# A graph layer on one core: row sums of two batches turned by one set of multiplications

## The chip, the cores and the metric

The kernel runs on one core of one Trainium2 chip. The metric is the device time in microseconds of one execution. It is compared with the time of the kernel before, run on the same chip.

## What is computed

```python
h = relu(layernorm(x))                       # x: 16 x 512 x 128
A = [A1, A2, shifted, A1.T, A2.T, shifted.T, eye]       # here A1 and A2 are both adj
HW = einsum('bnf,rfo->rbno', h, W[:, :F]) + einsum('rd,rdo->ro', W_edges, W[:, F:])[:, None, None, :]
AHW = einsum('rbnm,rbmo->rbno', A, HW)
out = x + max(AHW, axis=0) + b
```

There are 16 batches of 512 nodes with 128 features and seven relations r. `shifted` moves whole batches (`jnp.roll` on the batch axis of a stack of identity matrices), so it is the identity in each batch. The constant of each relation, multiplied by adj, becomes that constant times the row sum of adj (and, for the transposed relations, the row sum of its transpose).

## The kernel before

Everything lies with the 128 features on the partitions and the 512 nodes along the free dimension. Matrix products are made with float32r operands: each operand is split into a rounded part (`_hi`) and the rest (`_lo`), and three multiplications (hi by hi, hi by lo, lo by hi) give one product.

One batch passes through these steps. SP loads x, adj and adjT (each of the latter 1 MB), the bias, and stores the output. ACT makes a_hi from adj in four pieces (`split_adj`, L422) and aT_hi from adjT in four pieces (`split_adjT`, L431). Each piece also leaves the row sums of its 128 rows in `sums`. DVE makes a_lo and aT_lo of the first two pieces (L596, L603), POOL those of the last two (L334, L341). ACT makes h (L443) and h_hi (L449), DVE h_lo.

TensorE then computes, for batch b and in this order: gT = aggregate of h with adj into `bank_gT` (L808 to L818, 12 multiplications); the turn of h into `bank_p1` (L741); g = aggregate with adjT into `bank_g` (L832 to L841, 12 multiplications); the turn of the row sums into `bank_p2` (`turn_sums`, L749, four multiplications of 128 columns); the three products of h (`product`, i = 0 to 2, three multiplications each, L870 to L872) into bank_p0, 1 and 2; four small multiplications that start the other products with constant times row sum (`add_sums`, L860); the four products of gT and g. Product 2 overwrites bank_p2, so it waits until ACT has copied the turned sums out of it to `sumsT` (`copy_sumsT`, L473). The products with the sums wait for `sumsT` and for g_lo.

POOL writes the row sums into `sum_parts` (`part_sums`, L307 and L311): for each of the four 128-node pieces 128 columns, made of four groups of 32 (adj twice, adjT twice). In a group only the first four columns are filled: hi, lo, hi, lo. The turn puts those columns on partitions, and `c_rows`, 32 rows for each relation, has the rounded constant in two of the rows and its rest in the next two, and zero elsewhere.

ACT copies gT, hT and g out of PSUM as gT_hi, hT_hi and g_hi (L461, L455, L467), and DVE subtracts for the lo parts. ACT begins `best` with the first product (L480), and DVE takes the maximum with the other six (L637, L640). POOL adds x and bias (L327).

Each engine runs its own list of instructions in the order in which the code issues them. Semaphores join the lists. In the loop over b ACT's order is: split_adj(b+1), gT_hi(b), hT_hi(b), standard deviation (b+2), h(b+1), g_hi(b), sumsT(b), best(b), split_adjT(b+1). POOL's is: o_sb(b-1), a_lo and aT_lo of b+1, part_sums(b+1), bias DMA. SP's is: load x(b+3), load adj(b+2), store(b-1), load bias(b+1), load adjT(b+2). The adj load of a batch waits, among others, for gT of the batch two before (`gT_psum`), the adjT load for g of it (`g_psum`). Buffers of adj, adjT, their hi and lo parts, sums and sum_parts are double.

Of the kernel before, what the change touches and what calls it, by code (L numbers as in the profile page):

```python
# [5 lines left out]
ALU = mybir.AluOpType  # L6
# [5 lines left out]
P = 128  # L12
# [14 lines left out]
FIRST = 2  # L27
NX = 4


def gnn_kernel(nc: bass.Bass, x: bass.AP, xT: bass.AP, adj: bass.AP, adjT: bass.AP, W: bass.AP,
# [14 lines left out]
    with ExitStack() as ctx:  # L46
# [33 lines left out]


        sums = pair("sums", [P, 2, C])
        sum_parts = pair("sum_parts", [P, C, 2, 2, GROUP], F32R)
# [25 lines left out]
        c_col = sb("c_col", [P, R])  # L109
        row_hi = sb("row_hi", [P, 1])  # L110
        row_lo = sb("row_lo", [P, 1])
        c_hi = sb("c_hi", [P, O], F32R)
        c_rest = sb("c_rest", [P, O])
        c_low = sb("c_low", [P, O])
        c_rows = sb("c_rows", [P, O], F32R)

# [88 lines left out]
        def turns(b):  # L205

            return 16 * (b // 2 + 1)

        block = ctx.enter_context(nc.Block())

        @block.sync
        def _(sp):
# [19 lines left out]

            def load_adjT(b):
                q = b % 2
                if b >= 2:
                    if b - 2 < FIRST:
                        sp.wait_ge(sums_ready, 2 * (b - 2) + 2)
                    sp.wait_ge(g_psum, b - 1)
                if b >= 2 + FIRST:
                    sp.wait_ge(aThi_ready, (b - 1 - FIRST) * NS)  # L240
                    sp.wait_ge(aTlo_ready, (b - 1 - FIRST) * ND)
                if b > 2 + FIRST:
                    sp.wait_ge(aTlo_last_ready, (b - 2 - FIRST) * NG)
                sp.dma_start(adjT_sb[q][:, :, :], adjT_dram[b]).then_inc(adjT_in[q], 16)
# [50 lines left out]
        def _(pool):  # L295
            def part_sums(b):
                q = b % 2
# [12 lines left out]
                for copy in range(2):  # L310
                    last = nc.gpsimd.tensor_tensor(sum_parts[q][:, :, :, :, 2 * copy + 1], s,  # L311
                                                   sum_parts[q][:, :, :, :, 2 * copy].bitcast(F32), ALU.subtract)
                last.then_inc(parts_lo, 1)
# [74 lines left out]

        @block.scalar
        def _(act):  # L390
# [78 lines left out]
            def copy_sumsT(b):  # L469
                act.wait_ge(sumsT_psum, b + 1)  # L470
# [53 lines left out]
            for b in range(1, B):  # L524

                if 2 <= b < B - 1:
                    split_adj(b + 1)
                split_gT(b)
                split_hT(b)
                if 2 <= b < B - 2:  # L530
                    std_of(b + 2)
                if b + 1 < B:
                    make_h(b + 1)
                split_g(b)
                copy_sumsT(b)
                begin_best(b)
                if b == 1:
                    split_adj(b + 1)
                    std_of(b + 2)
                if b + 1 < B:  # L540
                    split_adjT(b + 1)

        @block.vector
        def _(dve):
# [77 lines left out]
            def split_g_lo(b):  # L622
                dve.wait_ge(ghi_ready, b + 1)
                nc.vector.tensor_tensor(g_lo[:, :], bank_g[:, 0:N], g_hi[:, :].bitcast(F32),
                                        ALU.subtract).then_inc(glo_ready, 1)

            def take_best(b, i):
                q = b % 2
# [16 lines left out]
            groups = ident[:, :].rearrange("p (g s) -> p g s", s=GROUP)  # L645
            nc.vector.tensor_reduce(row_hi[:, :], groups[:, :, 0:2], AXIS.XY, ALU.add)
            nc.vector.tensor_reduce(row_lo[:, :], groups[:, :, 2:4], AXIS.XY, ALU.add).then_inc(masks_ready, 1)
            first_variance(0, half_stats_done, half_aggr_done)
# [14 lines left out]
            for i, rels in enumerate((A_RELS, AT_RELS)):  # L663
# [16 lines left out]
                                    ALU.subtract).then_inc(c_step, 1)  # L680
            dve.wait_ge(masks_ready, 1)
            dve.wait_ge(c_step, 2)
            nc.vector.tensor_scalar(c_low[:, :], c_rest[:, :], row_lo[:, :], None, ALU.mult).then_inc(c_step, 1)
            dve.wait_ge(c_step, 3)
            nc.vector.scalar_tensor_tensor(out=c_rows[:, :], in0=c_hi[:, :].bitcast(F32), scalar=row_hi[:, :],
                                           in1=c_low[:, :], op0=ALU.mult, op1=ALU.add).then_inc(crow_ready, 1)
            split_g_lo(0)
            take_best(0, 1)
            take_best(0, 2)
# [45 lines left out]
        def _(pe):  # L735
# [8 lines left out]
            def turn_sums(b):  # L744
                pe.wait_ge(parts_lo, b + 1)
                if b >= 1:
                    pe.wait_ge(best_done, (b - 1) * NBEST + 2)
                for c in range(C):
                    last = nc.tensor.matmul(bank_s[:, c * P:(c + 1) * P],  # L749
                                            sum_parts[b % 2][:, c, :, :, :].rearrange("p d g k -> p (d g k)"),  # L750
                                            ident_r[:, :], start=True, stop=True)
                last.then_inc(sumsT_psum, 1)
# [92 lines left out]
            def begin_products(b):  # L845

                pe.wait_ge(sumsT_ready, b + 1)
                pe.wait_ge(crow_ready, 1)
                pe.wait_ge(glo_ready, b + 1)
                for i in range(NH, NPROD - int(b == B - 1)):  # L850
                    add_sums(i, bank_of[i], start=True)
                if b == B - 1:
                    pe.wait_ge(best_begun, B)
                    for nodes, to in zip(HALVES, last_banks):
                        add_sums(NPROD - 1, to, nodes, start=True)

            def add_sums(i, to, nodes=slice(0, N), start=False, stop=False):
                group = ORDER_A.index(ORDER[i])
                rows = slice(group * GROUP, (group + 1) * GROUP)
                return nc.tensor.matmul(to[:, nodes], c_rows[rows, :], sumsT[rows, nodes], start=start, stop=stop)  # L860

# [12 lines left out]
            def product(b, i, nodes=slice(0, N), to=None):  # L874
# [6 lines left out]
                if i == 2:  # L881
                    pe.wait_ge(sumsT_ready, b + 1)
                if i == 3:
# [4 lines left out]
            def products_first():  # L888
# [14 lines left out]
                for i in range(NH, NPROD):  # L903
                    add_sums(i, bank_of[i], stop=True).then_inc(prod_psum, 1)

# [12 lines left out]
            for b in range(1, B):  # L918
# [44 lines left out]
```

## Time and profile before

| | us |
|---|---|
| median of 3 runs | 205.33 (205.29 to 205.62) |
| profiled execution | 205.48 |
| its span | 203.7 |
| TensorE busy | 197.7 (97%) |
| DVE busy | 170.0 (83%) |
| ACT busy | 160.1 (79%) |
| POOL busy | 115.8 (57%) |

The span is what the profile shows of the execution from its first to its last instruction. Busy times overlap between engines. The chain that ended last is followed back from the last instruction, at each step to what released it; 94% of the span in it is TensorE.

### The profile page before, as it was taken

Reading aid. Unit: us, or ns where it says so; the run is one execution under the profiler, and the core shown is the slowest. Engines: PE = TensorE matmul, PEld = TensorE weight load, DVE = VectorE, ACT = ScalarE, POOL = GpSimd, SP = SyncE. Lnnn points to the kernel's source line nnn. Section 1 sums busy time; section 2 is a strip of 40 time slices with the busy share of each in tenths; the row PEclk is TensorE's granted clock in tenths of the full one; section 3 lists DMA queues with packets and bytes.
Section 4 is the critical chain, followed back from the end, with each engine's and each line's share of the span. In section 5 each row is a group of like instructions: output and inputs, shape, how many; then the busy total and the mean of one; then the engine's idle time right before and its main releaser. Section 6 shows DMA issues by size and latency. Waiting matters only on the chain.

```text
span 203.7 us, 3448 instructions
## 1 busy us (share of the span) xinstructions
PE 197.7 (97%) x918; PEld 151.2 (74%) x918; DVE 170.0 (83%) x411; ACT 160.1 (79%) x432; POOL 115.8 (57%) x162
## 2 busy tenths in 40 slices
PE   6999999999999999999999999999999999999991
PEld 6456466778787787878778787878878787887871
DVE  3487969989898998989989898998989899878565
ACT  3887989996969879696988969697896969795230
POOL 4041341477574938657592956759295675939500
PEclk9999999999999999999999999999999999999999
DMA  5999999997888979789987969799795969570501
GB/s 161 333 356 358 373 346 273 293 357 191 258 315 232 350 183 342 201 269 306 292 304 162 381 153 333 228 246 357 198 395 107 312 199 343 208 154 0 100 4 51
DMA packets 33748, 51.07 MB, mean 251 GB/s; under 512 B 1873, under 2 KB 11329, under 8 KB 33729
## 3 DMA queue, kind: packets, MB, share of 16 engines
q1 hardware_dynamic: 31152, 46.53, 67.1%
q0 software_dynamic: 2304, 4.20, 13.3%
q8 instruction: 7, 0.11, 0.2%
q10 hardware_dynamic: 272, 0.13, 0.2%
q14 instruction: 13, 0.10, 0.1%
HBM read 46.65 MB, written 4.19 MB: 250 GB/s over the span
## 4 chain that ended last, share of the span: by engine, by line
PE 94%; DMA 2%; DVE 2%; SPq 0%; issue 0%; DVEq 0%
PE bank_p L870 13%; PE bank_p L871 11%; PE bank_p L872 10%; PE bank_g L832 6%; PE bank_g L835 6%; PE bank_g L841 6%; PE bank_gT L818 6%; PE bank_gT L812 6%; PE bank_gT L808 6%; PE bank_p L741 3%; PE bank_p L860 3%; PE bank_p L749 3%; DMA adj_sb<-in_adj_dram 2%; PE bank_g L789 2%; PE bank_gT L780 2%; PE bank_g L770 2%
## 5 line engine op out<-in xcount | busy, mean ns | idle before, releaser
L334 POOL TENSOR_TENSOR a_lo<-adj_sb,a_hi 128x512 fp32r<-128x512 f32 x26 | 33.1, 1296 | 31.6 <-DVE a_lo L596 28.5
L640 DVE TENSOR_TENSOR best<-bank_p,best 128x512 f32<-128x512 f32 x48 | 33.1, 691 | 7.2 <-PE bank_p L872 6.0
L422 ACT ACTIVATE a_hi<-adj_sb 128x512 fp32r<-128x512 f32 x56 | 34.5, 620 | 1.3 <-DMA adj_sb<-in_adj_dram 1.3
L431 ACT ACTIVATE aT_hi<-adjT_sb 128x512 fp32r<-128x512 f32 x56 | 34.4, 620 | 0.0
L341 POOL TENSOR_TENSOR aT_lo<-adjT_sb,aT_hi 128x512 fp32r<-128x512 f32 x26 | 33.2, 1297 | 0.9 <-ACT aT_hi L431 0.3
L327 POOL TENSOR_TENSOR o_sb<-best,x_bias 128x512 f32<-128x512 f32 x15 | 19.8, 1317 | 19.1 <-DVE aT_lo L603 15.9
L637 DVE SCALAR_TENSOR_TENSOR best<-bank_p,c_col,best 128x512 f32<-128x512 f32 x32 | 24.0, 750 | 6.6 <-ACT best L480 6.0
L461 ACT ACTIVATE gT_hi<-bank_gT 128x512 fp32r<-128x512 f32 x16 | 9.5, 595 | 25.0 <-PE bank_gT L818 24.7
L443 ACT ACTIVATE h<-x_sb,shift,rstd 128x128 f32<-128x128 f32 x60 | 24.7, 488 | 0.0
L870 PE MATMUL bank_p<-hT_hi,w_hi 128*128 128x512 f32 x48 | 20.0, 417 | 0.0
L872 PE MATMUL bank_p<-hT_lo,w_hi 128*128 128x512 f32 x48 | 18.7, 390 | 0.0
L871 PE MATMUL bank_p<-hT_hi,w_lo 128*128 128x512 f32 x48 | 18.7, 389 | 0.0
L596 DVE TENSOR_TENSOR a_lo<-adj_sb,a_hi 128x512 fp32r<-128x512 f32 x28 | 18.0, 683 | 0.0
L603 DVE TENSOR_TENSOR aT_lo<-adjT_sb,aT_hi 128x512 fp32r<-128x512 f32 x28 | 17.9, 681 | 0.0
L319 POOL DMA_DIRECT2D x_bias<-in_xT_dram x16 | 13.8, 863 | 5.0 <-DMA x_bias<-in_biasT_dram 4.6
L832 PE MATMUL bank_g<-aT_hi,h_hi 128*128 128x512 f32 x54 | 16.3, 422 | 0.0
L808 PE MATMUL bank_gT<-a_hi,h_hi 128*128 128x512 f32 x54 | 14.9, 397 | 0.0
L835 PE MATMUL bank_g<-aT_hi,h_lo 128*128 128x512 f32 x54 | 14.7, 392 | 0.0
L841 PE MATMUL bank_g<-aT_lo,h_hi 128*128 128x512 f32 x54 | 14.6, 390 | 0.0
L818 PE MATMUL bank_gT<-a_lo,h_hi 128*128 128x512 f32 x54 | 14.6, 390 | 0.0
L812 PE MATMUL bank_gT<-a_hi,h_lo 128*128 128x512 f32 x54 | 14.5, 389 | 0.0
L619 DVE TENSOR_TENSOR gT_lo<-bank_gT,gT_hi 128x512 fp32r<-128x512 f32 x16 | 11.1, 691 | 3.8 <-ACT gT_hi L461 2.8
(122 smaller groups left out, 477.7 us busy)
## 6 DMA issues: line engine op xcount, KB each, us to landing
adj_sb<-in_adj_dram SPq DMA_DIRECT2D x15, 1024.0 KB, 7.5
adjT_sb<-in_adjT_dram SPq DMA_DIRECT2D x15, 1024.0 KB, 8.3
x_bias<-in_biasT_dram SPq DMA_DIRECT2D x16, 256.0 KB, 6.5
x_bias<-in_xT_dram POOLq DMA_DIRECT2D x16, 256.0 KB, 4.1
x_sb<-in_x_dram SPq DMA_DIRECT2D x15, 256.0 KB, 8.3
out_dram<-o_sb SPq DMA_DIRECT2D x15, 256.0 KB, 5.5
adj_sb<-in_adj_dram SPq DMA_DIRECT2D x4, 256.0 KB, 5.1
adjT_sb<-in_adjT_dram SPq DMA_DIRECT2D x4, 256.0 KB, 5.1
```

The source lines that it names most:

```text
L334: nc.gpsimd.tensor_tensor(a_lo[q][:, c, :], adj_sb[q][:, c, :], a_hi[q][:, c, :].bitcast(F32), ALU.subtract).then_inc(alo_last_ready, 1)
L341: nc.gpsimd.tensor_tensor(aT_lo[q][:, c, :], adjT_sb[q][:, c, :], aT_hi[q][:, c, :].bitcast(F32), ALU.subtract).then_inc(aTlo_last_ready, 1)
L422: nc.scalar.activation(a_hi[q][:, c, :], adj_sb[q][:, c, :], ACT.Copy, accum_out=sums[q][:, 0, c:c + 1]).then_inc(ahi_ready, 1)
L431: nc.scalar.activation(aT_hi[q][:, c, :], adjT_sb[q][:, c, :], ACT.Copy, accum_out=sums[q][:, 1, c:c + 1]).then_inc(aThi_ready, 1)
L640: op = nc.vector.tensor_tensor(best[q][:, :], product, best[q][:, :], ALU.max)
L808: nc.tensor.matmul(bank_gT[:, 0:N], h_hi[q][:, c, :], a_hi[q][:, c, :], start=(c == 0 and b > FIRST), stop=False)
L818: last = nc.tensor.matmul(bank_gT[:, 0:N], h_hi[q][:, c, :], a_lo[q][:, c, :], start=False, stop=(c == split_chunks(b)[-1]))
L832: nc.tensor.matmul(bank_g[:, 0:N], h_hi[q][:, c, :], aT_hi[q][:, c, :], start=(c == 0 and b > FIRST), stop=False)
L835: nc.tensor.matmul(bank_g[:, 0:N], h_lo[q][:, c, :], aT_hi[q][:, c, :], start=False, stop=False)
L870: nc.tensor.matmul(dst, w_hi[:, i, :], hi[:, nodes], start=start, stop=False)
L871: nc.tensor.matmul(dst, w_lo[:, i, :], hi[:, nodes], start=False, stop=False)
L872: return nc.tensor.matmul(dst, w_hi[:, i, :], lo[:, nodes], start=False, stop=stop)
```

## The change

From batch 3 on, batches are taken in pairs (3, 4), (5, 6), ... (13, 14). In the first of a pair POOL fills, beside its own row sums, those of the next batch into columns 4 to 7 of each group of 32, and the one turn of that batch carries both. In the second of a pair there is no turn and no copy of sumsT; its products with the sums use a second set `c_rows[1]`, whose constants stand in rows 4 to 7 of each group. For this the row sums of the next batch must exist earlier: in the first of a pair ACT splits adjT of the next batch directly after adj, ahead of gT_hi, and POOL fills the parts ahead of its share of the splits. SP issues the adjT load directly behind the adj load, and from the load of batch 5 on neither waits for gT_psum or g_psum.

```diff
+PAIRED = 3
...
+        def leads(b):
+
+            return b >= PAIRED and (b - PAIRED) % 2 == 0 and b + 1 < B
+
+        def follows(b):
+            return b >= 1 and leads(b - 1)
+
+        def turn_of(b):
+
+            return b if b < PAIRED else PAIRED + (b - PAIRED) // 2
...
-                    sp.wait_ge(gT_psum, b - 1)
+                    if b - 2 <= FIRST:
+                        sp.wait_ge(gT_psum, b - 1)
...
-                    sp.wait_ge(g_psum, b - 1)
+                    if b - 2 <= FIRST:
+                        sp.wait_ge(g_psum, b - 1)
...
                     load_adj(b + 2)
+                    load_adjT(b + 2)
                 store(b - 1)
                 if b + 1 < B:
                     load_bias(b + 1)
-                if b + 2 < B:
-                    load_adjT(b + 2)
...
-                if b >= 2:
-                    pool.wait_ge(sumsT_psum, b - 1)
+                if turn >= 2:
+                    pool.wait_ge(sumsT_psum, turn - 1)
+                parts = sum_parts[turn % 2]
                 for copy in range(2):
-                    last = nc.gpsimd.tensor_copy(sum_parts[q][:, :, :, :, 2 * copy], s)
+                    last = nc.gpsimd.tensor_copy(parts[:, :, :, :, first + 2 * copy], s)
...
                 finish(b - 1)
+                if leads(b):
+                    part_sums(b + 1)
...
-                    part_sums(b + 1)
+                    if not leads(b):
+                        part_sums(b + 1)
...
                     split_adj(b + 1)
+                if leads(b):
+                    split_adjT(b + 1)
                 split_gT(b)
...
-                copy_sumsT(b)
+                if not follows(b):
+                    copy_sumsT(b)
...
-                if b + 1 < B:
+                if b + 1 < B and not leads(b):
                     split_adjT(b + 1)
...
             split_g_lo(0)
+            rows_of_c(1)
             take_best(0, 1)
...
             def turn_sums(b):
-                pe.wait_ge(parts_lo, b + 1)
+                pe.wait_ge(parts_lo, b + 1 + int(leads(b)))
...
-                pe.wait_ge(sumsT_ready, b + 1)
-                pe.wait_ge(crow_ready, 1)
+                pe.wait_ge(sumsT_ready, turn_of(b) + 1)
+                pe.wait_ge(crow_ready, 1 + int(follows(b)))
...
-                turn_sums(b)
+                if not follows(b):
+                    turn_sums(b)
```

The order of ACT's instructions in the first pair, kernel before, from the split of adjT of batch 3 (it is issued at the end of batch 2's turn through the loop) through batch 3. The number behind a name is the buffer.

```order
L431 ACTIVATE aT_hi1,sums1<-adjT_sb1 128x512 x4
L422 ACTIVATE a_hi0,sums0<-adj_sb0 128x512 x4
L461 ACTIVATE gT_hi<-bank_gT 128x512
L455 ACTIVATE hT_hi<-bank_p1 128x512
L395 ACTIVATE std1<-mean_var1,eps 128x4
L443 ACTIVATE h0<-x_sb2,shift0,rstd0 128x128 x4
L449 ACTIVATE h_hi0<-h0 128x512
L467 ACTIVATE g_hi<-bank_g 128x512
L473 ACTIVATE sumsT<-bank_p2 128x512
L480 ACTIVATE best1<-bank_p0,c_col 128x512
L431 ACTIVATE aT_hi0,sums0<-adjT_sb0 128x512 x4
L422 ACTIVATE a_hi1,sums1<-adj_sb1 128x512 x4
```

The same stretch of a later pair in the changed kernel (line numbers are those of the changed kernel: 449 is split_adjT, 440 split_adj, 479 gT_hi, 491 sumsT, 498 best).

```order
L449 ACTIVATE aT_hi1,sums1<-adjT_sb1 128x512 x4
L440 ACTIVATE a_hi0,sums0<-adj_sb0 128x512 x4
L449 ACTIVATE aT_hi0,sums0<-adjT_sb0 128x512 x4
L479 ACTIVATE gT_hi<-bank_gT 128x512
L473 ACTIVATE hT_hi<-bank_p1 128x512
L413 ACTIVATE std1<-mean_var1,eps 128x4
L461 ACTIVATE h0<-x_sb2,shift0,rstd0 128x128 x4
L467 ACTIVATE h_hi0<-h0 128x512
L485 ACTIVATE g_hi<-bank_g 128x512
L491 ACTIVATE sumsT<-bank_p2 128x512
L498 ACTIVATE best1<-bank_p0,c_col 128x512
L440 ACTIVATE a_hi1,sums1<-adj_sb1 128x512 x4
```

The split of adjT for the next batch has moved from behind best to ahead of gT_hi; in the first of a pair twelve instead of eight split pieces stand in a row.

SP's list in the steady part of the kernel before, with what each row waits for:

```order
L231 DMA adj_sb<-in_adj_dram 128x4x512 [waits alo_ready,alo_last_ready,ahi_ready,gT_psum]
L254 DMA out_dram<-o_sb 128x512 [waits out_ready]
L250 DMA x_bias<-in_biasT_dram 128x512 [waits out_ready]
L244 DMA adjT_sb<-in_adjT_dram 128x4x512 [waits aTlo_ready,aTlo_last_ready,aThi_ready,g_psum]
L218 DMA x_sb<-in_x_dram 128x4x128 [waits h0_scaled,h_ready]
```

And in the changed kernel (245 loads adj, 259 adjT, 269 stores, 265 loads the bias, 231 loads x):

```order
L245 DMA adj_sb<-in_adj_dram 128x4x512 [waits alo_last_ready,alo_ready,ahi_ready]
L259 DMA adjT_sb<-in_adjT_dram 128x4x512 [waits aTlo_last_ready,aTlo_ready,aThi_ready]
L269 DMA out_dram<-o_sb 128x512 [waits out_ready]
L265 DMA x_bias<-in_biasT_dram 128x512 [waits out_ready]
L231 DMA x_sb<-in_x_dram 128x4x128 [waits h0_scaled,h_ready]
```

The adjT load stands ahead of store and bias load, and the waits for the two aggregates are gone.

## Rows read from the trace of the kernel before

**Rows 1.** The page: TensorE's busy time, and its granted clock in 40 slices.

```profile
PE 197.7 (97%) x918; PEld 151.2 (74%) x918; DVE 170.0 (83%) x411; ACT 160.1 (79%) x432; POOL 115.8 (57%) x162
...
PEclk9999999999999999999999999999999999999999
```

**Rows 2.** Chain that ended last, in order of time: start us, us, what.

```profile
75.69 0.40 PE bank_p L749 x4
76.08 0.29 PE bank_p L870
...
79.04 0.23 PE bank_p L871
```

**Rows 3.** Timeline of TensorE, batch 5: start us, duration us, line, operation.

```profile
76.43 0.39 PE L872 MATMUL bank_p<-hT_lo,w_hi 128*128 128x512 f32 x1
...
77.34 0.39 PE L870 MATMUL bank_p<-hT_hi,w_hi 128*128 128x512 f32 x1
```

**Rows 4.** Timeline of ACT, batch 5 and the start of batch 6.

```profile
72.51 0.60 ACT L461 ACTIVATE gT_hi<-bank_gT 128x512 fp32r<-128x512 f32 x1 [1.35 <-PE bank_gT L818]
...
76.36 0.59 ACT L473 ACTIVATE sumsT<-bank_p 128x512 fp32r<-128x512 f32 x1
76.86 0.69 ACT L480 ACTIVATE best<-bank_p,c_col 128x512 f32<-128x512 f32 x1
77.44 0.62 ACT L431 ACTIVATE aT_hi<-adjT_sb 128x512 fp32r<-128x512 f32 x1
...
84.31 0.60 ACT L461 ACTIVATE gT_hi<-bank_gT 128x512 fp32r<-128x512 f32 x1 [1.54 <-PE bank_gT L818]
```

**Rows 5.** Timeline of ACT, around the start of batch 3.

```profile
42.06 0.62 ACT L431 ACTIVATE aT_hi<-adjT_sb 128x512 fp32r<-128x512 f32 x1
...
44.52 0.62 ACT L422 ACTIVATE a_hi<-adj_sb 128x512 fp32r<-128x512 f32 x1
...
48.93 0.60 ACT L461 ACTIVATE gT_hi<-bank_gT 128x512 fp32r<-128x512 f32 x1 [1.87 <-PE bank_gT L818]
```

**Rows 6.** Timeline of ACT, batch 0.

```profile
17.24 0.60 ACT L473 ACTIVATE sumsT<-bank_p 128x512 fp32r<-128x512 f32 x1 [1.02 <-PE bank_p L749]
```

**Rows 7.** Timeline of TensorE's weight loads, batches 0 and 5.

```profile
17.89 0.19 PEld L870 LDWEIGHTS bank_p<-hT_hi,w_hi 128*128 128x128 f32 x1 [0.17 <-ACT sumsT L473]
...
75.30 0.64 PEld L749 LDWEIGHTS bank_p<-ident_r,sum_parts 128*128 128x128 f32 x4
```

**Rows 8.** Timeline of POOL, batch 5.

```profile
73.14 1.29 POOL L327 TENSOR_TENSOR o_sb<-best,x_bias 128x512 f32<-128x512 f32 x1 [1.32 <-DVE aT_lo L603]
...
81.95 0.34 POOL L307 CAST sum_parts<-sums 128x16 fp32r<-128x16 f32 x2
...
82.76 0.84 POOL L319 DMA_DIRECT2D x_bias<-in_xT_dram  x1
```

**Rows 9.** Timeline of DVE, batch 5.

```profile
76.62 0.68 DVE L624 TENSOR_TENSOR g_lo<-bank_g,g_hi 128x512 fp32r<-128x512 f32 x1
77.62 1.54 DVE L637 SCALAR_TENSOR_TENSOR best<-bank_p,c_col,best 128x512 f32<-128x512 f32 x2 [0.31 <-ACT best L480]
79.61 2.14 DVE L640 TENSOR_TENSOR best<-bank_p,best 128x512 f32<-128x512 f32 x3 [0.45 <-PE bank_p L872]
```

**Rows 10.** Timeline of DVE, batch 0.

```profile
15.22 0.86 DVE L683 TENSOR_SCALAR c_low<-c_rest,row_lo 128x128 f32<-128x128 f32 x1
16.12 0.35 DVE L685 SCALAR_TENSOR_TENSOR c_rows<-c_hi,row_hi,c_low 128x128 fp32r<-128x128 f32 x1
...
18.45 1.54 DVE L637 SCALAR_TENSOR_TENSOR best<-bank_p,c_col,best 128x512 f32<-128x512 f32 x2 [1.38 <-ACT best L480]
```

**Rows 11.** Timeline of SP's queue, batch 2: the load of adjT for batch 4.

```profile
40.70 0.42 SPq L244 DMA_DIRECT2D adjT_sb<-in_adjT_dram  x1
```

**Rows 12.** Time to landing of adjT loads: issued at 40.70 and at 76.03.

```profile
DMA to landing us min/median/max: 7.6/7.6/7.6
...
DMA to landing us min/median/max: 9.7/9.7/9.7
```

More of the change, by code:

```diff
@@ L109, in gnn_kernel @@
         c_col = sb("c_col", [P, R])
-        row_hi = sb("row_hi", [P, 1])
-        row_lo = sb("row_lo", [P, 1])
+        row_hi = sb("row_hi", [P, 2])
+        row_lo = sb("row_lo", [P, 2])
         c_hi = sb("c_hi", [P, O], F32R)
         c_rest = sb("c_rest", [P, O])
-        c_low = sb("c_low", [P, O])
-        c_rows = sb("c_rows", [P, O], F32R)
+        c_low = pair("c_low", [P, O])
+        c_rows = pair("c_rows", [P, O], F32R)
         bank_gT = bank("bank_gT")
@@ L296, in part_sums @@
             def part_sums(b):
-                q = b % 2
+                q, turn, first = b % 2, turn_of(b), 4 * int(follows(b))
                 s = sums[q][:, :, :].rearrange("p d c -> p c d").unsqueeze(3).to_broadcast([P, C, 2, 2])
@@ L310, in part_sums @@
                 for copy in range(2):
-                    last = nc.gpsimd.tensor_tensor(sum_parts[q][:, :, :, :, 2 * copy + 1], s,
-                                                   sum_parts[q][:, :, :, :, 2 * copy].bitcast(F32), ALU.subtract)
+                    last = nc.gpsimd.tensor_tensor(parts[:, :, :, :, first + 2 * copy + 1], s,
+                                                   parts[:, :, :, :, first + 2 * copy].bitcast(F32), ALU.subtract)
                 last.then_inc(parts_lo, 1)
@@ L469, in copy_sumsT @@
             def copy_sumsT(b):
-                act.wait_ge(sumsT_psum, b + 1)
+                act.wait_ge(sumsT_psum, turn_of(b) + 1)
                 if b >= 1:
@@ L625, in split_g_lo, with rows_of_c @@
                                         ALU.subtract).then_inc(glo_ready, 1)
+            def rows_of_c(s):
+                dve.wait_ge(masks_ready, 1)
+                dve.wait_ge(c_step, 2)
+                nc.vector.tensor_scalar(c_low[s][:, :], c_rest[:, :], row_lo[:, s:s + 1], None,
+                                        ALU.mult).then_inc(c_step, 1)
+                dve.wait_ge(c_step, 3 + s)
+                nc.vector.scalar_tensor_tensor(out=c_rows[s][:, :], in0=c_hi[:, :].bitcast(F32),
+                                               scalar=row_hi[:, s:s + 1], in1=c_low[s][:, :], op0=ALU.mult,
+                                               op1=ALU.add).then_inc(crow_ready, 1)
             def take_best(b, i):
@@ L645, in _ @@
             groups = ident[:, :].rearrange("p (g s) -> p g s", s=GROUP)
-            nc.vector.tensor_reduce(row_hi[:, :], groups[:, :, 0:2], AXIS.XY, ALU.add)
-            nc.vector.tensor_reduce(row_lo[:, :], groups[:, :, 2:4], AXIS.XY, ALU.add).then_inc(masks_ready, 1)
+            for s in range(2):
+                nc.vector.tensor_reduce(row_hi[:, s:s + 1], groups[:, :, 4 * s:4 * s + 2], AXIS.XY, ALU.add)
+                last = nc.vector.tensor_reduce(row_lo[:, s:s + 1], groups[:, :, 4 * s + 2:4 * s + 4], AXIS.XY, ALU.add)
+            last.then_inc(masks_ready, 1)
             first_variance(0, half_stats_done, half_aggr_done)
@@ L680, in _ @@
                                     ALU.subtract).then_inc(c_step, 1)
[L681 to L686, printed above, removed]
+            rows_of_c(0)
             split_g_lo(0)
+            rows_of_c(1)
             take_best(0, 1)
@@ L749, in turn_sums @@
                     last = nc.tensor.matmul(bank_s[:, c * P:(c + 1) * P],
-                                            sum_parts[b % 2][:, c, :, :, :].rearrange("p d g k -> p (d g k)"),
+                                            sum_parts[turn_of(b) % 2][:, c, :, :, :].rearrange("p d g k -> p (d g k)"),
                                             ident_r[:, :], start=True, stop=True)
@@ L845, in begin_products @@
             def begin_products(b):
-                pe.wait_ge(sumsT_ready, b + 1)
-                pe.wait_ge(crow_ready, 1)
+                pe.wait_ge(sumsT_ready, turn_of(b) + 1)
+                pe.wait_ge(crow_ready, 1 + int(follows(b)))
                 pe.wait_ge(glo_ready, b + 1)
                 for i in range(NH, NPROD - int(b == B - 1)):
-                    add_sums(i, bank_of[i], start=True)
+                    add_sums(b, i, bank_of[i], start=True)
                 if b == B - 1:
@@ L854, in begin_products, with add_sums @@
                     for nodes, to in zip(HALVES, last_banks):
-                        add_sums(NPROD - 1, to, nodes, start=True)
-            def add_sums(i, to, nodes=slice(0, N), start=False, stop=False):
+                        add_sums(b, NPROD - 1, to, nodes, start=True)
+            def add_sums(b, i, to, nodes=slice(0, N), start=False, stop=False):
                 group = ORDER_A.index(ORDER[i])
                 rows = slice(group * GROUP, (group + 1) * GROUP)
-                return nc.tensor.matmul(to[:, nodes], c_rows[rows, :], sumsT[rows, nodes], start=start, stop=stop)
+                return nc.tensor.matmul(to[:, nodes], c_rows[int(follows(b))][rows, :], sumsT[rows, nodes], start=start, stop=stop)
             def passes(i, dst, nodes=slice(0, N), start=False, stop=False):
@@ L881, in product @@
                 if i == 2:
-                    pe.wait_ge(sumsT_ready, b + 1)
+                    pe.wait_ge(sumsT_ready, turn_of(b) + 1)
                 if i == 3:
@@ L903, in products_first @@
                 for i in range(NH, NPROD):
-                    add_sums(i, bank_of[i], stop=True).then_inc(prod_psum, 1)
+                    add_sums(0, i, bank_of[i], stop=True).then_inc(prod_psum, 1)
             pe.wait_ge(ident_ready, 1)
```

## The prediction

> **What bounds the kernel now.** I read the page first. TensorE is busy for 97% of the span at a granted clock of nine tenths or more in every slice, that is at its 2.4 GHz level [rows 1], so only what shortens or stalls TensorE moves the time. Then the chain that ended last, in order of time: in the steady part it is one unbroken run of TensorE pieces, with no wait in it, and each batch takes 11.80 us (gT_hi is copied at 72.51 and at 84.31, [rows 4]). So nothing else is late today, and the question is which engine becomes late once its order changes. For that I read the timelines of ACT, POOL and DVE around batch 5, and ask of each result that TensorE consumes how long before its use it is ready.
>
> I call batches 3, 5, ... 13 the leads and 4, 6, ... 14 the followers: six pairs. Batches 0 to 2 and 15 keep the old scheme.
>
> **Removed: the turn of the row sums, once in each follower.** Four small multiplications (L749) hold 0.40 us of the chain, and the product behind them holds 0.29 us where an ordinary one holds 0.23 us [rows 2]. That extra 0.06 us belongs to the change of shape and I expect most of it to go too. The removal is worth 0.40 to 0.46 us; I take 0.45, since a product follows products' shape there. Six times 0.45 is **2.7 us**. In the follower ACT also loses one copy of sumsT (0.50 us from 76.36 to 76.86, [rows 4]), which was not on the chain.
>
> A rule of the Trainium skill speaks against this term. The rows show 0.10 us for each 128-column multiplication at the full clock [rows 1, 2]; the page "TensorE: Matmul & The Clock Gate", section "Back-to-back issue gap", prices one at N/2.4 + 2.5 ns, about 56 ns, so that four would be an estimated 0.22 us. By the rows the term is 2.7 us, by the page 1.3 us. The measured row decides for my sum.
>
> **Added to the leads: ACT splits adjT of the next batch before it splits gT.** This is where the gain can be lost, so it is followed step by step. I move the rows of batches 5 and 6 as if 5 were a follower and 6 a lead.
>
> Follower: gT_hi starts at 72.51 as before. The slot of the sumsT copy (76.36) now goes to best, which waits for the first product. That product's last multiplication starts at 76.43 and lasts 0.39 [rows 3]; with 0.45 us less ahead of it, it ends at 76.37, and best starts 0.04 us behind it at 76.41, as it does today (76.82 and 76.86). 0.58 us later (76.86 to 77.44, [rows 4]) ACT starts the split of adjT for the lead: 76.99. A split of four pieces without a wait occupies 2.46 us (42.06 to 44.52, [rows 5]). So ACT starts the lead's split of adj at 79.45, the added split of adjT at 81.91, and is free at 84.37. In the lead gT is complete at 84.31 - 0.45 = 83.86. ACT reaches it **0.51 us late**. The second pair of rows gives the same for the first lead: 44.52 + 2 x 2.46 = 49.44 against 48.93 [rows 5], again 0.51 us.
>
> All that ACT does next moves by 0.51 us: hT_hi, h, h_hi, g_hi, then sumsT. TensorE's third product needs bank_p2, from which sumsT is copied, so it waits for that copy. Today the copy starts at 76.36 and takes 0.59 us, so it ends at 76.95, and the third product starts at 77.34 [rows 3, 4]. How much of the 0.39 us between is slack is read where this wait did bite, in batch 0: the copy starts at 17.24 and takes 0.60, and the weight load of the third product begins at 17.89, 0.05 us after its end [rows 6, 7]. Between a late weight load and its multiplication I allow 0.06 to 0.10 us. The slack is therefore about 0.24 us, and 0.51 - 0.24 = 0.27 us remain as a stall of TensorE. A restart like the one behind L749 costs another 0.03 to 0.06 us (0.29 against 0.23, [rows 2]), so I take **0.31 us in each lead, 1.9 us in all**. Its bounds: none, if the copy has 0.3 us more slack than I see, and 0.45 us, which is the whole saving. The chain of ACT starts anew at gT_psum in every follower, where it idles, so the delay does not add up from pair to pair.
>
> **The other consumers in a lead.** hT_lo and gT_lo come at most 0.51 us later, more than 0.5 us before their use. g_lo on DVE starts at 76.62 and lasts 0.68 [rows 9]; moved by 0.51 to 0.55 us it ends at 77.85, before the products with the sums. best is begun 0.51 us later, so DVE's two takes (77.62, 1.54 us for both) end at 79.67, against 79.61 plus the stall, when the next product is ready [rows 9]. DVE gets no new bound.
>
> **POOL: row parts of the next batch moved ahead of its adj split, in a lead.** Behind it wait the split of a_lo and aT_lo, where POOL idled. Ahead of it stands o_sb: it starts at 73.14, when DVE's aT_lo is done, and takes 1.29 us; the row parts then take 0.81 us (81.95 to 82.76) [rows 8]. They are ready at 75.24, and the weight load of the turn starts at 75.30 [rows 7]. No wait, by 0.06 us only. A delay here up to 0.3 us costs nothing: it shifts TensorE toward the later sumsT and takes the place of the stall. I cost it at nothing. The parts also need ACT's last piece of adjT, which ends well before o_sb does.
>
> **Loads.** The adj load no longer waits for gT_psum, and the adjT load is issued directly behind it, ahead of the store and of the bias load; what stands behind it on SP is the store, which waits for a later event anyway. The adjT load is now held only by DVE's aT_lo, done at about 73.1 [rows 8], and in the example it is needed at 81.91: it has 8.8 us. It took 9.7 us in the slowest steady case and 7.6 us in another [rows 12], each behind a store and a bias load that now come after it. I expect about 7 us, no wait. The first lead is tighter: its load was issued at 40.70 [rows 11] and keeps its wait for g_psum, so it goes at about 40.35; with the old 7.6 us it lands at 47.95, with the store and bias load behind it about 1.2 us sooner. ACT wants it at 44.52 + 2.46 = 46.98. Cost between 0 and 0.97 us, once; I take 0.
>
> **Startup.** The second set of c_rows is two more DVE instructions, 0.86 and 0.35 us by their twins, put into a stretch in which DVE idled 1.38 us before its first take [rows 10]. Two more small reductions run while DVE waits for x. Both nothing; if the cover failed, about 0.2 us once.
>
> **Sum.** -2.7 + 1.9 + 0 = -0.8 us. The profiled execution took 205.48 us with a span of 203.7; the median of the runs is 205.33, 0.15 us lower. So the span should become 202.9 and the median **204.5 us**.
>
> **Rivals.**
>
> *No stall.* If the third product has enough slack, or ACT keeps up, only the removal counts: 205.33 - 2.7 = 202.6. For it: sumsT has 0.39 us before its use. Against it: ACT is 0.51 us late by two separate pairs of rows. 14%.
>
> *The stall eats the saving.* At 0.45 us in each lead nothing is left: 205.3. The restart cost is my least certain term. 12%.
>
> *The first lead alone is late.* adjT(4) lands at 47.95 instead of before 46.98: 0.97 us once, and the time is 205.33 - 0.8 + 0.97 = 205.5. 10%.
>
> *Late adjT in every lead, slower than before.* The load needs 9.7 us as in the slowest case, and ACT waits 0.9 us more in front of gT. Then the stall is 1.2 us, each pair loses 0.75 us, and the time is 205.33 + 4.5 = 209.8. It turns to a loss once the load takes more than 8.8 + 0.14 = 8.9 us from issue. Against it: the two 256 KB transfers ahead are gone and adj is issued earlier. 10%.
>
> *The turn was cheaper than its piece of the chain.* If 128 columns cost a quarter of the 0.23 us of 512, the four hold only 0.23 us of real work and the rest is a change of weights that stays. With the stall of 0.31 this gives 6 x 0.08 = +0.5 us, 205.8. 6%, since the chain counts 0.40 in every batch. The rule of the Trainium skill named above would favour this case.
>
> My forecast has 48%.
>
> **How the numbers follow.** A measurement of this kernel can tell 0.2%, 0.41 us, from no change. Faster: forecast and no stall, 0.62. Same: the stall that eats the saving and the first lead alone, 0.22. Slower: the last two, 0.16. The range from 202.6 to 205.9 takes in all but the late load in every lead.
>
> **What would show it.** On TensorE ten turns of the sums should be left of sixteen. In a lead, the weight load of the third product should stand behind ACT's sumsT with a wait of about 0.3 us, six times, and nowhere else; ACT's wait for gT should be zero in leads and about 4 us in followers, since adjT is split there already. If the third product does not wait, the rival without stall is right. If ACT shows a wait for DMA before aT_hi in leads, the load is late. If the follower's period is 11.4 and the lead's 12.1, the sum is right. The prediction is wrong if ACT's four pieces take other than 2.46 us, or if POOL's row parts come more than 0.3 us late.

## The result: 0.65% slower

The changed kernel takes 206.76 us (median of 4 runs, 206.65 to 207.25), the kernel before 205.48 us beside it. The ratio is 1.0065 with a 95% interval of 1.005 to 1.008. The prediction was 204.5 us with a range up to 205.9 us: wrong in sign, and outside its range. One execution in each of two experiments below fell into a slower state of the chip, and medians and ranges leave it out. The ratios and their intervals are worked out from all those executions, not from the two medians, and can differ from the quotient of the medians by up to 0.2%.

The page of the changed kernel answers [rows 1]. TensorE is as busy as before, for less work, and the chain that ended last now leaves it:

```profile
PE 197.5 (97%) x894; PEld 148.2 (72%) x894; DVE 170.7 (83%) x415; ACT 156.0 (76%) x426; POOL 115.7 (57%) x162
...
PE 78%; DMA 8%; ACT 5%; DVE 4%; issue 3%; POOL 0%; ACTq 0%; DVEq 0%; POOLq 0%; SPq 0%
```

TensorE's busy share of 97% does not show where the stalls are, since the waits on this path stand at the weight loads. The waits of the changed kernel, longest in total (engine and line, waited for, us in total, times, longest), show them (of POOL's 13.1 us the longest wait, 4.7, lies at the start and is there before the change too, with 4.6):

```profile
POOL x_bias L334 <- DMA x_bias<-in_biasT_dram: 13.1, 7, 4.7
...
PEld bank_p L900 <- ACT sumsT L491: 3.1, 7, 0.6
...
PEld bank_p L779 <- POOL sum_parts L326: 1.7, 2, 1.3
...
ACT aT_hi L449 <- DMA adjT_sb<-in_adjT_dram: 1.6, 2, 1.3
```

In the trace of before the only wait of this kind on TensorE was the one of batch 0 [rows 7]; there were none for POOL's row parts or for adjT in the steady part.

The clearest view is one worked out from the timelines: the time from the first multiplication of a batch's gT with the rounded parts to the same of the next batch. Leads stand in bold for the kernels that have pairs.

| batch | 2 | 3 | 4 | 5 | 6 | 7 | 8 | 9 | 10 | 11 | 12 | 13 | 14 |
|---|---|---|---|---|---|---|---|---|---|---|---|---|---|
| before | 11.19 | 11.80 | 11.78 | 11.80 | 11.78 | 11.80 | 11.78 | 11.80 | 11.78 | 11.80 | 11.78 | 11.80 | 11.78 |
| changed | 11.31 | **13.37** | 11.33 | **12.09** | 11.33 | **12.54** | 11.32 | **12.08** | 11.33 | **12.08** | 11.33 | **12.09** | 11.33 |

A follower gains 0.45 us, six times out of six. A lead loses 0.29 us in four of six. Batch 3 loses 1.57 us, batch 7 0.74 us, batch 2 0.12 us. The sum of the losses and gains is 3.57 - 2.71 = +0.86 us, which is the 0.9 us by which the span grew (203.7 to 204.6).

**Outside the span.** The profiled execution of the changed kernel took 206.65 us, 2.05 us more than its span, where before it was 1.8 us. These 0.3 us are no accident of one execution. In all 40 executions of kernels with six pairs (this one and those of five experiments below) the time outside the span is 2.0 to 2.1 us; in all 36 executions of the variants with five pairs or none, and in those of the kernel before, it is 1.7 to 1.8 us. What causes it is not shown, since the profile covers only the span.

**An undisturbed lead, batch 11.** ACT's timeline (start, duration, engine and line, operation), to be read beside [rows 4]. Neither aT_hi nor gT_hi has a wait in front of it.

```profile
142.47 0.62 ACT L449 ACTIVATE aT_hi<-adjT_sb 128x512 fp32r<-128x512 f32 x1
...
144.92 0.58 ACT L479 ACTIVATE gT_hi<-bank_gT 128x512 fp32r<-128x512 f32 x1
...
148.76 0.59 ACT L491 ACTIVATE sumsT<-bank_p 128x512 fp32r<-128x512 f32 x1
```

The weight load of the third product in the same batch:

```profile
149.40 0.19 PEld L900 LDWEIGHTS bank_p<-hT_hi,w_hi 128*128 128x128 f32 x1 [0.40 <-ACT sumsT L491]
```

The copy ends at 149.35 and the load starts 0.05 us later, as in batch 0 [rows 6, 7]. This part is as predicted: 3.84 us from gT_hi to sumsT, and a lead that is 0.29 us longer.

**Batch 3.** The chain that ended last goes back from there to one transfer, and ACT's timeline shows the wait at its end:

```profile
40.33 8.01 DMA adjT_sb<-in_adjT_dram
...
54.18 0.37 ACT g_hi L485
54.65 0.60 ACT sumsT L491
```

```profile
48.36 0.63 ACT L449 ACTIVATE aT_hi<-adjT_sb 128x512 fp32r<-128x512 f32 x1 [1.30 <-DMA adjT_sb<-in_adjT_dram]
...
50.83 0.58 ACT L479 ACTIVATE gT_hi<-bank_gT 128x512 fp32r<-128x512 f32 x1
```

gT_hi starts at 50.83 where it started at 48.93 [rows 5]. At the same time POOL waited for the bias load, which now stands behind adjT in SP's queue, and its bias DMA stands ahead of o_sb and the row parts:

```profile
50.01 0.87 POOL L334 DMA_DIRECT2D x_bias<-in_xT_dram  x1 [1.93 <-DMA x_bias<-in_biasT_dram]
50.61 1.59 POOL L342 TENSOR_TENSOR o_sb<-best,x_bias 128x512 f32<-128x512 f32 x1
51.85 0.63 POOL L322 CAST sum_parts<-sums 128x16 fp32r<-128x16 f32 x2
52.56 0.44 POOL L326 TENSOR_TENSOR sum_parts<-sums,sum_parts 128x16 fp32r<-128x16 f32 x2
```

So the turn of the sums starts late too, and then the third product once more:

```profile
53.05 0.52 PEld L779 LDWEIGHTS bank_p<-ident_r,sum_parts 128*128 128x128 f32 x4 [1.27 <-POOL sum_parts L326]
...
55.29 0.19 PEld L900 LDWEIGHTS bank_p<-hT_hi,w_hi 128*128 128x128 f32 x1 [0.57 <-ACT sumsT L491]
```

Batch 7 shows the same two in small: the adjT load issued at 86.43 took 9.2 us, ACT waited 0.35 us for it, and POOL 1.25 us for the bias load. The six loads that a lead waits for, from batch 3 on, landed in 8.0, 5.9, 9.2, 6.3, 5.5 and 5.5 us; from batch 9 on neither wait appears in a lead.

### The profile page after: what moved, and what is told of

Its sections match the earlier page's. It is cut to its first block, busy times and chain, and to the rows that moved or that the text cites. A ratio compares the mean times of both kernels' runs of the same rounds, so it can differ in the third digit from the quotient of the medians.

```text
span 204.6 us, 3365 instructions
## 1 busy us (share of the span) xinstructions
PE 197.5 (97%) x894; PEld 148.2 (72%) x894; DVE 170.7 (83%) x415; ACT 156.0 (76%) x426; POOL 115.7 (57%) x162
## 4 chain that ended last, share of the span: by engine, by line
PE 78%; DMA 8%; ACT 5%; DVE 4%; issue 3%; POOL 0%; ACTq 0%; DVEq 0%; POOLq 0%; SPq 0%
PE bank_p L900 11%; PE bank_p L902 9%; PE bank_p L901 8%; DMA adjT_sb<-in_adjT_dram 8%; PE bank_g L862 5%; PE bank_g L865 5%; PE bank_g L871 5%; PE bank_gT L848 5%; PE bank_gT L842 5%; PE bank_gT L838 5%; PE bank_p L890 3%; PE bank_p L771 3%; DVE best L672 2%; PE bank_p L938 2%; PE bank_gT L793 2%
## 5 line engine op out<-in xcount | busy, mean ns | idle before, releaser
L342 POOL TENSOR_TENSOR o_sb<-best,x_bias 128x512 f32<-128x512 f32 x15 | 20.6, 1376 | 15.1 <-DVE aT_lo L624 8.2
L334 POOL DMA_DIRECT2D x_bias<-in_xT_dram x16 | 13.9, 866 | 13.1 <-DMA x_bias<-in_biasT_dram 13.1
```

## Experiments

The theory after the result: the gain (0.45 us in a follower) and the stall (0.29 us in a lead) are as predicted, and the rest is lost where a load comes late, mostly in batch 3. The rivals: the new load order itself costs, with or without pairs; POOL's queue, not ACT, carries the delay; or the turn was not worth its 0.45 us.

### What a turn is worth

```diff
-                for c in range(C):
+                for c in list(range(C)) * (2 if b >= 3 and b % 2 == 0 else 1):
```

in `turn_sums` of the kernel before. The results are unchanged, since the four multiplications only write again what they wrote.

> The kernel before with the four multiplications of the turn issued twice in batches 4, 6, ... 14. By the chain one turn holds 0.40 us: +2.4 us, 207.9 us. If the turn is mostly a change of weights and 128 columns are worth about 0.06 us each: +1.3 us, 206.8 us.

Measured: 208.56 us, ratio 1.0146 (1.0126 to 1.0167). The batches with the second turn take 12.23 or 12.22 us where they took 11.78; all others are as before. A turn adds 0.44 or 0.45 us, 0.11 us a piece. That is near the chain's 0.40 us, and the estimate of 0.06 us a piece does not hold. The six of them make 2.7 us; the rest of the 2.9 us between the medians lies outside the span (1.8 to 1.95 us in the four executions, 1.7 to 1.8 before).

### The loads alone

```diff
-PAIRED = 3
+PAIRED = 15
```

in the changed kernel: there is no pair left.

> The changed kernel with no pair at all: only the order and the gates of the loads are new. My theory (the loss comes from what the leads need early, not from the loads as such): within 0.2% of the kernel before, 205.1 to 205.9 us. Rival (the new load order itself costs the 1.3 us, through contention or the later bias load): 206.5 to 207 us.

Measured: 206.2 us against 205.7, ratio 1.0029 (1.0013 to 1.0044). Between the two expectations, so neither holds: the loads alone cost some 0.6 us. It is all at the start: batch 2 takes 11.91 us and batch 3 11.87, the others as before. The waits name the step, and the timelines of DVE and POOL the reason:

```profile
PE bank_p L890 <- DVE g_lo L645: 0.6, 1, 0.6
```

```profile
39.68 1.18 DVE L610 SCALAR_TENSOR_TENSOR shift<-mean_var,rstd 128x4 f32<-128x4 f32 x1
```

```profile
38.66 0.86 POOL L334 DMA_DIRECT2D x_bias<-in_xT_dram  x1 [2.96 <-DMA x_bias<-in_biasT_dram]
39.27 1.57 POOL L342 TENSOR_TENSOR o_sb<-best,x_bias 128x512 f32<-128x512 f32 x1
```

`shift` handles four numbers in each partition and normally takes 0.16 us. Here it takes 1.18 us and ends at 40.86, when POOL's o_sb ends (40.84). The early load of adjT for batch 3 pushed the bias load back, this held POOL's bias DMA for 2.96 us and o_sb behind it, and o_sb now lies where DVE makes shift. Everything behind shift on DVE comes 1 us late, g_lo last. In the changed kernel's own profile the same instruction took 0.60 us and cost batch 2 0.12 us.

All the traces together bear this out. In the five with the early load of adjT for batch 3, shift of this batch took 0.60, 0.88, 0.89, 1.14 and 1.18 us, and batch 2 took 11.31, 11.60, 11.63, 11.87 and 11.91 us: beyond some 0.3 us of slack this batch pays every lengthening in full. In the other nine shift took 0.16 us and batch 2 took 11.19 to 11.22 us.

### Without the first pair

```diff
-PAIRED = 3
+PAIRED = 5
```

in the changed kernel, so that the pairs are (5, 6) to (13, 14).

> The changed kernel with pairs only from batch 5 on, so without the lead of batch 3. Theory (in batch 3 the adjT load lands 1.3 us after ACT wants it, a leftover of the busy start, and that alone costs 1.4 us there): the pair's own -0.45 + 0.28 us are lost, the 1.4 us are saved, 205.4 to 205.8 us. Rival (any first lead pays, since the backlog of loads follows): batch 5 waits instead and the time stays at 206.5 to 207 us.

Measured: 205.37 us, ratio 0.9977 (0.9962 to 0.9992). Batch 5 takes 12.09 us, like every lead in this run (12.08 to 12.16), and ACT never waits for adjT. The lateness belongs to batch 3 and does not follow the first lead. Batch 2 took 11.87 us here, the loss of the run above.

### POOL's bias DMA behind the row parts

```diff
                 if leads(b):
                     part_sums(b + 1)
+                    add_bias(b)
...
-                    add_bias(b + 1)
+                    if not leads(b + 1):
+                        add_bias(b + 1)
```

in the changed kernel.

> The changed kernel with POOL's bias DMA for a lead moved behind the row parts, so that a late bias load no longer holds o_sb and the row parts in POOL's queue. Theory (the late adjT load reaches the third product through ACT by itself; POOL's delay lies beside it): no change, 206.5 to 207.0 us, and the turn of batch 3 starts earlier while the third product does not. Rival (POOL's wait for the bias load is the cause): 205.2 to 205.9 us.

Measured: 207.16 us, ratio 1.0063 (1.0039 to 1.0088), the same as the changed kernel. Batch 3 took 13.97 us in this execution, in which adjT came later still:

```profile
ACT aT_hi L451 <- DMA adjT_sb<-in_adjT_dram: 2.2, 1, 2.2
```

The turn and the third product of batch 3 show which of the two waits counts:

```profile
53.76 0.52 PEld L781 LDWEIGHTS bank_p<-ident_r,sum_parts 128*128 128x128 f32 x4 [0.80 <-POOL sum_parts L326]
...
57.09 0.19 PEld L902 LDWEIGHTS bank_p<-hT_hi,w_hi 128*128 128x128 f32 x1 [1.27 <-ACT sumsT L493]
```

Counted from the first multiplication of the batch's gT (47.29 here, 46.12 in the changed kernel), the turn starts after 6.47 us instead of 6.93, and the third product after 9.80 instead of 9.17, directly behind sumsT. The turn came sooner and the third product did not, as expected. So the rival falls: in batch 3 POOL's wait for the bias load lies beside ACT's wait for adjT. Batch 7 took 12.11 us here, without its excess; one execution cannot say whether that is the edit.

### Early adjT only where a lead needs it

```diff
                     load_adj(b + 2)
-                    load_adjT(b + 2)
+                    if follows(b + 2):
+                        load_adjT(b + 2)
                 store(b - 1)
                 if b + 1 < B:
                     load_bias(b + 1)
+                if b + 2 < B and not follows(b + 2):
+                    load_adjT(b + 2)
```

once with the pairs from batch 5, once with those from batch 3.

> Pairs from batch 5 on, and the adjT load ahead of store and bias load only where a lead needs it; all other loads keep the order of the kernel before. Theory (the early adjT load at the start pushes the bias load, POOL's bias DMA and o_sb back until DVE's small shift instruction runs into o_sb, 0.7 us in batch 2): batch 2 takes 11.2 us again, five pairs at -0.45 + 0.29 give -0.8, 204.7 us. Rival (the 0.7 us come from the loads of adj and adjT themselves): 205.4 us as in the run without the first pair.

Measured: 204.6 us, ratio 0.9949 (0.9933 to 0.9964). Batch 2 takes 11.19 us again, shift 0.16 us, and the rest is the sum of pairs. In this run's timelines shift starts when the shorter and earlier o_sb is all but done (39.60, o_sb ends at 39.66):

```profile
39.60 0.16 DVE L613 SCALAR_TENSOR_TENSOR shift<-mean_var,rstd 128x4 f32<-128x4 f32 x1
```

```profile
38.37 1.29 POOL L345 TENSOR_TENSOR o_sb<-best,x_bias 128x512 f32<-128x512 f32 x1 [1.41 <-DVE aT_lo L627]
```

> The changed kernel with its six pairs from batch 3, and the early adjT load only where a lead needs it, so that the load for batch 3 and the bias load behind it keep their old order. Theory (the lateness in batch 3 is made partly by the change itself, which lets the bias DMA of batch 2 fall beside the adjT load of batch 4): that load lands at least 0.7 us sooner and batch 3 takes 12.1 to 12.7 us instead of 13.4; 204.5 to 205.1 us. Rival (the start's backlog alone): batch 3 takes 13.4 us or more, 205.7 us or more.

Measured: 204.95 us (nine executions, 204.39 to 206.5), ratio 0.9969 (0.9944 to 0.9993). In the profiled execution the load for batch 4 landed in 7.5 us instead of 8.0, ACT waited 0.79 us, and batch 3 took 12.98 us:

```profile
48.37 0.63 ACT L452 ACTIVATE aT_hi<-adjT_sb 128x512 fp32r<-128x512 f32 x1 [0.79 <-DMA adjT_sb<-in_adjT_dram]
```

The load came 0.5 us sooner, not 0.7, and the batch lies between the two expected values. But this execution, at 206.2 us, is one of the slowest of the nine. Their median span is 202.9 us, 1.2 us below that of the kernel before beside it (204.1), and six undisturbed pairs save 2.7 - 1.7 = 1.0 us. A typical execution therefore has no room for 0.9 us lost in batch 3: there the old order of the load for batch 3 seems to remove most of the lateness, not a part of it. No trace of such an execution was taken. This version beats the kernel before by a little; its spread (2.1 us) is wide, like those of the pairs from batch 4 and of the old load order below.

### The old order of the loads

In the changed kernel the adjT load goes back behind store and bias load in every batch; pairs stay, and so do the waits of the loads as the change left them.

> The changed kernel with the adjT load put back behind the store and the bias load; the pairs and the new gates stay. Theory (a lead needs adjT some 9 us after DVE's aT_lo releases its buffer, and a load takes 8 to 9 us): issued some 2 us later it lands about 1.8 us after ACT wants it, in every lead, so each pair loses 1.6 us: about 214 us, at least 209. Rival (what hurts is that the bias load now stands behind adjT): 205 to 206 us.

Measured: 208.40 us (three executions, 207.31 to 209.74), ratio 1.0137 (1.0081 to 1.0192). Right in sign, but far less than 214 and below the 209 that was expected at least. The leads of batches 3 and 7 took 14.02 and 13.43 us, and the other four 12.08 to 12.16, no more than with the early load. ACT waited only twice:

```profile
ACT aT_hi L450 <- DMA adjT_sb<-in_adjT_dram: 3.1, 2, 1.9
```

The issue did move as expected: the load that the lead of batch 5 waits for goes out at 66.26 and is wanted at 72.58, so it has 6.3 us where it had 8.8 (62.99 to 71.78). Wrong were the 8 to 9 us that I took for a load. The six that a lead waits for took 8.2, 6.0, 7.7, 6.5, 6.2 and 6.2 us, and all but the first and the third were in time. The adj load, freed of gT_psum, has landed by then (issued at 58.58, 5.2 us), where before the change it was still under way; that this makes them short is not shown. In this execution the early issue matters in batches 3 and 7.

### Copying the sums first

In a lead, pairs from batch 5:

```diff
+                if leads(b):
+                    copy_sumsT(b)
                 split_g(b)
-                if not follows(b):
+                if leads(b):
+                    round_h(b + 1)
+                elif not follows(b):
                     copy_sumsT(b)
```

where `round_h` is the last step of `make_h` (h_hi). On DVE, g_lo of a lead goes ahead of h_lo. The loads are those of the changed kernel.

> Pairs from batch 5 on with the load order of the changed kernel. In a lead ACT copies sumsT directly after h and rounds h only after g_hi; DVE makes g_lo ahead of h_lo. Theory (the 0.28 us of a lead are the third product waiting for the copy of sumsT): the wait is gone in five leads, 205.4 - 1.4 = 204.0 us, and a lead takes 11.8 us. Rival (ACT's 0.5 us come back at the next consumer, g_lo or best): a lead still takes 12.1 us and the time is 205.4 us.

Measured: 204.11 us (203.39 to 204.86), ratio 0.9912 (0.9882 to 0.9942). The leads of batches 5 to 11 take 11.80 or 11.81 us, and in them nothing waits for sumsT. ACT's timeline of batch 7 shows that the copy now waits for the turn instead of the other way round:

```profile
98.32 1.64 ACT L461 ACTIVATE h<-x_sb,shift,rstd 128x128 f32<-128x128 f32 x4
100.29 0.60 ACT L494 ACTIVATE sumsT<-bank_p 128x512 fp32r<-128x512 f32 x1 [0.32 <-PE bank_p L789]
```

ACT is still half a microsecond late for gT_hi, and nothing pays for it. Batches 2 and 3 took 11.60 and 12.27 us, the loss that the early load makes at the start (shift took 0.88 and 1.44 us). One lead, batch 13, took 12.40 us: POOL's late bias DMA again held up o_sb and the row parts behind it:

```profile
166.04 0.88 POOL L334 DMA_DIRECT2D x_bias<-in_xT_dram  x1 [1.07 <-DMA x_bias<-in_biasT_dram]
166.70 1.55 POOL L342 TENSOR_TENSOR o_sb<-best,x_bias 128x512 f32<-128x512 f32 x1
```

### The mends together

The order above and the early adjT for leads' followers only, pairs from batch 5:

> Pairs from batch 5 on, the early adjT load only where a lead needs it, and in a lead the copy of sumsT directly after h (ACT) and g_lo ahead of h_lo (DVE). The two mends measured so far should add up: 204.6 us of the run with the loads mended, less five stalls of 0.28 us: 203.2 us. If they do not add up: 204.0 us or more.

Measured: 203.28 us (202.98 to 203.74), ratio 0.987 (0.9843 to 0.9896). The two mends add up to what was expected. The leads take 11.80, 11.80, 11.80, 11.93 and 11.84 us, the followers 11.32 or 11.33.

The same with POOL's bias DMA behind the row parts in a lead:

```diff
                     part_sums(b + 1)
+                    add_bias(b)
...
-                    add_bias(b + 1)
+                    if not leads(b + 1):
+                        add_bias(b + 1)
```

> The same, and POOL's bias DMA of a lead behind the row parts. Theory (what is left of lost time is a single late bias load holding o_sb and the row parts in some lead): 203.2 us with a narrower spread. Rival (the later bias DMA delays the next o_sb): above 203.6 us.

Measured: 203.69 us (203.31 to 203.82), ratio 0.9886 (0.9866 to 0.9905). All five leads take 11.80 us, as the theory has it, but the time is above 203.6, as the rival has it. The profiled executions show where it went: batches 2 to 14 together took 150.40 us against 150.62 without this edit, and batch 2 began at 35.34 instead of 34.76, ahead of anything that the edit touches. This start varies over the traces from 34.70 to 35.71 us. The total is not lower than without the edit; the intervals overlap.

Without that edit, and with one pair more:

```diff
-PAIRED = 5
+PAIRED = 4
```

> Both mends together and the pairs (4,5) to (14,15), six of them. Theory: six times -0.45 us with no stall and no loss at the start, 202.8 us. If the stall only moves to another consumer: 204.5 us. If the first lead is late again for adjT: about 1 us more than either.

Measured: 204.05 us (203.35 to 206.11), ratio 0.9928 (0.9903 to 0.9954). In the profiled execution, the slowest of them, batch 6 took 13.54 us. There POOL's late bias DMA held up o_sb and the row parts:

```profile
85.34 0.86 POOL L337 DMA_DIRECT2D x_bias<-in_xT_dram  x1 [1.68 <-DMA x_bias<-in_biasT_dram]
85.95 1.58 POOL L345 TENSOR_TENSOR o_sb<-best,x_bias 128x512 f32<-128x512 f32 x1
87.19 1.63 POOL L325 CAST sum_parts<-sums 128x16 fp32r<-128x16 f32 x2
```

All three edits, with the pairs from batch 4:

> The six pairs (4,5) to (14,15) with all three mends. In the run without the third mend one lead waited 1.9 us for the row parts behind a late bias DMA. Theory (that wait goes): 202.8 us, and no lead above 11.9 us. Rival (the row parts are late for another reason): 204 us as before.

Measured: 203.69 us (203.3 to 203.75), ratio 0.9884 (0.9865 to 0.9904). No lead takes more than 11.84 us, and the spread of ten runs from 203.35 to 206.11 has shrunk to 0.45 us in four. In the profiled execution with 206.11 us above, POOL's queue was the cause by its timeline, unlike in batch 3. That the edit cures such a case was not tried: in this run's profiled execution no bias load was late in a lead. The sixth pair brings nothing measurable in all: the mean span is 201.5 us against 201.9 with five pairs, and the time outside the span 2.1 us against 1.75.

## Why the prediction was wrong

**What bounds the kernel**: right within the span. Every difference in the table is a stall or a removal on TensorE.

**The removal**: right. 0.45 us predicted, 0.45 us measured in each follower, 0.44 us for each turn added. The doubt drawn from the Trainium skill, "TensorE: Matmul & The Clock Gate", section "Back-to-back issue gap", was settled by both: its 56 ns for 128 columns did not hold for this turn, at 0.10 to 0.11 us a piece. The section gives that formula for a single isolated multiplication, and about 81 ns for a stream in which each has its weight load; I had used only the first. The turn lies above both.

**The stall in a lead**: right in mechanism, place and size. 0.31 us predicted, 0.29 us measured, and gone when the copy came first. The weight load's wait itself read 0.40 us in the undisturbed leads, not 0.3. The rival without a stall and the one in which the stall eats the saving are both excluded.

**Startup**: right. Batch 2 begins at 34.81 us, before the change at 34.82.

**The loads**: this step failed, in three ways. First, for the lead of batch 3 I named a cost between 0 and 0.97 us and took 0, because store and bias load would stand behind adjT and I subtracted 1.2 us for them. The load was issued at 40.33 as expected and took 8.0 us, more than the 7.6 us of [rows 12]. ACT waited 1.30 us, beyond my upper end, and batch 3 lost 1.28 us more than another lead. I took the old landing for an upper bound, while the same change also let the bias DMA of batch 2 run later, beside this load; the version with the early load for followers only makes it likely that this was most of the lateness. Second, the same reasoning failed in batch 7, for 0.45 us: its load took 9.2 us where there were 8.8. The rival of the late load (9.7 us, and a loss from 8.9 us on) had this mechanism and expected it in every lead, and it came in one. Of the other four my 7 us were on the safe side (5.5 to 6.3).

Third, I asked of each moved load only who waits for it, and not who waits for the load it was moved past. The bias load is waited for by POOL's bias DMA, behind which stand o_sb and, in a lead, the row parts. I wrote that the row parts come 0.06 us before their use and that only DVE's aT_lo holds o_sb. Both were read from an execution in which the bias load was on time. In batches 3 and 7 the turn waited 1.27 and 0.44 us for the row parts, more than the 0.3 us that the prediction itself named as a sign of being wrong. Without this the loss in batch 2 (0.7 us in the run with the loads alone) has no place in my sum.

**The sum**: -0.8 us predicted, +0.9 us in the span. The difference of 1.7 us is 1.28 in batch 3, 0.45 in batch 7 and 0.12 in batch 2, less about 0.1 us of stalls that were smaller than forecast. To this come the 0.3 us outside the span: I had carried the time outside it over unchanged, without a reason, and six pairs come with 0.3 us more of it. Why stays open. The rival of the first lead alone (205.5 us) named the right mechanism and was too small.

## What to carry to other kernels

When a load is moved ahead of others in one queue, follow those others too: the small bias load that was passed held up POOL, and POOL's next instruction held up DVE. A landing time from the old order is no upper bound for the new one. And an engine that falls behind by half a microsecond need not cost anything: it cost 0.29 us until the one result that was waited for was made first.

## What was not expected of the hardware

DVE's `shift`, an operation on 128x4 numbers with two inputs in SBUF, does not end before POOL's running o_sb: 0.16 us alone, 1.18 us when it started 0.41 us after o_sb. The ends agree within 0.02 us in this run (40.86 and 40.84), and in the changed kernel's own profile, where o_sb ends at 38.66 + 1.59 = 40.25:

```profile
39.67 0.60 DVE L610 SCALAR_TENSOR_TENSOR shift<-mean_var,rstd 128x4 f32<-128x4 f32 x1
```

The Trainium skill, "SBUF — State Buffer", section "Who interferes with whom", says that an instruction of VectorE with both inputs in SBUF contends with one of GpSimd that reads SBUF, through a shared pair of ports that works as an exclusive lock. The traces agree. In nine cases, in six traces, shift started 0.17 to 1.33 us after o_sb, took 0.28 to 1.44 us, and ended 0.02 to 0.04 us after it. Two neighbours on DVE that have only one input in SBUF keep their usual times inside the same o_sb of the changed kernel (38.66 to 40.25):

```profile
38.88 0.68 DVE L635 TENSOR_TENSOR hT_lo<-bank_p,hT_hi 128x512 fp32r<-128x512 f32 x1
39.47 0.16 DVE L608 RECIPROCAL rstd<-std 128x4 f32<-128x4 f32 x1
```

The other direction is seen in the row parts of the run with pairs from batch 4: two casts that take 0.34 us [rows 8] took 1.63 us, while DVE worked on a_lo, whose inputs both lie in SBUF (87.48 to 88.76). That the two engines exclude each other was read from these ends, not tried by an experiment of its own.
